# Two matmuls instead of three for the modulation of a gated recurrence: the high and low weight columns in one tile of 34, the pairs of rows added by ScalarE and VectorE

## The reference

```
x = x + L0(x)     # gated recurrence, the layer of the change
x = x + L1(x)     # one linear layer per sequence, weights chosen by index
x = x + L2(x)     # adapter with layernorm, weights chosen by index
x = x + L3(x)     # one linear layer per sequence, weights chosen by index

def L0(x):        # E = 512 channels, D = 2 traces
    ctx      = causal_ema(x, tau_ctx)
    wg       = sigmoid([x, ctx] @ Wg.T + bg)
    gated    = x * wg
    h1       = gelu(x @ Wn1.T + bn1)                 # 128 channels
    mod      = 0.5 + sigmoid(h1 @ Wn2.T + bn2)       # D = 2 values a token
    traces   = causal_ema(gated * mod[..., d], tau_d)   for d in 0, 1
    temporal = sum over d of traces[d] * softmax(blend)[d]
    gate     = sigmoid(temporal @ Wtemp.T + btemp)
    soma     = gelu(x @ Wsoma.T + bsoma)
    return layernorm((soma * gate) @ Wout.T)
```

## Time and profile before

| | |
|---|---|
| median of 3 runs | 731.97 us (731.63 to 732.11) |
| the profiled execution's own time | 731.42 us |
| its span, first to last instruction | 729.6 us |
| granted TensorE clock over the span | 1.000 of full speed (the 2.4 GHz level) |
| PE busy | 721.6 us, 99% |
| DVE busy | 539.2 us, 74% |
| ACT busy | 371.7 us, 51% |
| POOL busy | 121.6 us, 17% |
| DMA, mean over the span | 128 GB/s |

### The profile page before, as it was taken

How to read it: one execution, slowest core, us unless ns; L and a number is a source line. 1 busy time by engine, 2 the same in 40 slices (tenths; PEclk the granted TensorE clock), 3 DMA queues, 4 the chain that set the end, 5 groups by cost and what they waited for, 6 DMA issues and landing times. The chain is left out here.

```text
span 729.6 us, 10095 instructions
## 1 busy us (share of the span) xinstructions
PE 721.6 (99%) x3317; PEld 594.9 (82%) x3317; DVE 539.2 (74%) x808; ACT 371.7 (51%) x554; POOL 121.6 (17%) x220
## 2 busy tenths in 40 slices
PE   9999999999999999999999999999999999999998
PEld 8887888888888888888888888888887878888886
DVE  5799796695596597587578569875988687677583
ACT  4365446445535535545544543656566475374540
POOL 2000030031013004004004015205212012021110
PEclk9999999999999999999999999999999999999999
DMA  7959307935943962960980861724444636433312
GB/s 201 256 126 180 61 1 110 192 75 91 191 94 66 193 115 50 180 144 17 184 173 0 155 221 50 267 99 162 146 134 153 167 99 197 123 112 98 87 73 86
DMA packets 119310, 93.54 MB, mean 128 GB/s; under 512 B 75583, under 2 KB 103262, under 8 KB 117230
## 3 DMA queue, kind: packets, MB, share of 16 engines
q1 hardware_dynamic: 112718, 86.56, 49.7%
q10 hardware_dynamic: 6368, 6.59, 3.1%
q0 software_dynamic: 192, 0.00, 0.1%
HBM read 32.28 MB, written 25.20 MB: 79 GB/s over the span
## 5 line engine op out<-in xcount | busy, mean ns | idle before, releaser
L685 PE MATMUL pc<-x_h,wg_h 128*128 128x512 f32 x224 | 87.5, 391 | 1.2 <-DVE s_l L1766 1.1
L687 PE MATMUL pc<-x_h,wg_l 128*128 128x512 f32 x224 | 87.2, 389 | 0.0
L686 PE MATMUL pc<-x_l,wg_h 128*128 128x512 f32 x224 | 87.2, 389 | 0.0
L1565 DVE TENSOR_TENSOR_SCAN stage_b<-alpha,carry,stage_b 128x512 f32<-128x512 f32 x64 | 78.5, 1268 | 0.0
L685 PEld LDWEIGHTS pc<-x_h,wg_h 128*128 128x128 f32 x224 | 42.1, 188 | 11.6 <-issue 1.6
L1198 ACT ACTIVATE ctx_t<-ctx_t,col_all 128x512 f32<-128x512 f32 x32 | 23.2, 724 | 54.9 <-DVE ctx_t L1545 54.8
L803 PE MATMUL pm<-t_h,wt_h 128*128 128x512 f32 x128 | 50.2, 392 | 0.6 <-DVE t_l L1578 0.5
L685 PE MATMUL pm<-wo_h,s_h 128*128 128x512 f32 x128 | 50.0, 390 | 0.0
L805 PE MATMUL pm<-t_h,wt_l 128*128 128x512 f32 x128 | 49.9, 390 | 0.0
L804 PE MATMUL pm<-t_l,wt_h 128*128 128x512 f32 x128 | 49.8, 389 | 0.0
L687 PE MATMUL pm<-wo_h,s_l 128*128 128x512 f32 x128 | 49.8, 389 | 0.0
(11 more groups left out here) (280 smaller groups left out, 1880.1 us busy)
## 6 DMA issues: line engine op xcount, KB each, us to landing
x_planes<-x_pairs SPq DMA_DIRECT2D x56, 256.0 KB, 6.9
xt_scratch<-x_t SPq DMA_DIRECT2D x8, 1024.0 KB, 9.9
n_scratch<-stage_a SPq DMA_DIRECT2D x8, 1024.0 KB, 9.5
ctx_t<-xt_scratch SPq DMA_DIRECT2D x16, 512.0 KB, 7.1
x_pairs<-n_scratch SPq DMA_DIRECT2D x14, 512.0 KB, 6.0
out_dram<-x_tok SPq DMA_DIRECT2D x28, 256.0 KB, 2.4
mod<-mod_scratch ACTq DMA_DIRECT2D x8, 512.0 KB, 3.6
x_planes<-stage_b SPq DMA_DIRECT2D x60, 64.0 KB, 2.0
```

Of the source, the lines that this page charges most:

```text
L685: nc.tensor.matmul(acc, ah, bh, start=start and q == 0, stop=False)
L686: nc.tensor.matmul(acc, ah, bl, start=False, stop=False)
L687: last = nc.tensor.matmul(acc, al, bh, start=False, stop=stop and q == n - 1)
L1565: nc.vector.tensor_tensor_scan(tr[:, m % 2, :], alpha[:, 1 + d:2 + d].to_broadcast([P, BLK]), tr[:, m % 2, :], carry[:, D - d, m:m + 1], A ...
```

## The change

The weights of the modulation, two columns, are laid into one tile `wn2` of 34 columns: the high parts in columns 0 and 1, zeros in 2 to 31, the low parts in 32 and 33. One matmul with the high part of the hidden activation and one with its low part then give 34 rows of `pt[0]`: rows 0 and 1 hold what the high weights give, rows 32 and 33 what the low weights give (now also low by low, which was left out before). ScalarE copies rows 32 and 33 to `h1` (`mod_low`), VectorE adds rows 0 and 1 to them (`mod_add`), and `mod_tanh` works on the sum in `h1`. `h1_product` of the next block waits for that sum instead of the tanh. VectorE waits for `ident` near its start, since the zeros are made from it.

```
-        wn2_h, wn2_l = sb("wn2_h", [P, D], F32R), sb("wn2_l", [P, D], F32R)
+        wn2 = sb("wn2", [P, 32 + D], F32R)
...
+        mod_part, mod_sum = sem("mod_part"), sem("mod_sum")
...
             def h1_product(i):
...
-                after(pe, mod_raw, i)
+                after(pe, mod_sum, i)
...
             def mod_product(i):
                 pe.wait_ge(h1_hi, i + 1)
                 pe.wait_ge(h1_lo, i + 1)
-                product(pt[0][0:D, :], [(wn2_h[:, :], wn2_l[:, :], h_h[:, :], h_l[:, :])]).then_inc(mod_mm, 1)
+
+                rows = pt[0][0:32 + D, :]
+                nc.tensor.matmul(rows, wn2[:, :], h_h[:, :], start=True, stop=False)
+                nc.tensor.matmul(rows, wn2[:, :], h_l[:, :], start=False, stop=True).then_inc(mod_mm, 1)
...
+            def mod_low(i):
+
+                act.wait_ge(mod_mm, i + 1)
+                nc.scalar.activation(h1[0:D, :], pt[0][32:32 + D, :], ACT.Identity).then_inc(mod_part, 1)
+
             def mod_tanh(i):
 
-                act.wait_ge(mod_mm, i + 1)
-                nc.scalar.activation(h1[0:D, :], pt[0][0:D, :], ACT.Tanh, bias=col_bn2[0:D, 0:1],
+                act.wait_ge(mod_sum, i + 1)
+                nc.scalar.activation(h1[0:D, :], h1[0:D, :], ACT.Tanh, bias=col_bn2[0:D, 0:1],
                                      scale=0.5).then_inc(mod_raw, 1)
...
             def step(i, last=False):
                 gates(i - 1, lambda: hidden(i))
+                mod_low(i)
                 mod_tanh(i)
...
+            mod_low(0)
             mod_tanh(0)
...
-            gates(0, lambda: (mod_tanh(1), mod_to_dram(1)))
+            gates(0, lambda: (mod_low(1), mod_tanh(1), mod_to_dram(1)))
...
+            def mod_add(i):
+                dve.wait_ge(mod_part, i + 1)
+                nc.vector.tensor_tensor(h1[0:D, :], pt[0][0:D, :], h1[0:D, :], ALU.add).then_inc(mod_sum, 1)
+
...
             def step(i, last=False):
                 gates(i - 1, lambda: hidden_lo(i))
-                for c in range(NC):
-                    scan_context(i, c)
+                scan_context(i, 0)
+                scan_context(i, 1)
+                mod_add(i)
+                scan_context(i, 2)
+                scan_context(i, 3)
                 traces_part(i, last)
...
+            dve.wait_ge(setup_done, 1)
...
-            nc.vector.tensor_scalar(wn2_h[:, :], col_wn2[:, :], 1.0, None, ALU.mult).then_inc(setup_v, 1)
-            dve.wait_ge(setup_v, 9 + D)
-            nc.vector.tensor_tensor(wn2_l[:, :], col_wn2[:, :], f32(wn2_h[:, :]), ALU.subtract).then_inc(consts_v, 1)
+            nc.vector.tensor_scalar(wn2[:, 0:D], col_wn2[:, :], 1.0, None, ALU.mult).then_inc(setup_v, 1)
+            nc.vector.tensor_scalar(wn2[:, D:32], ident[:, D:32], 0.0, None, ALU.mult).then_inc(setup_v, 1)
+            dve.wait_ge(setup_v, 10 + D)
+            nc.vector.tensor_tensor(wn2[:, 32:32 + D], col_wn2[:, :], f32(wn2[:, 0:D]), ALU.subtract).then_inc(consts_v, 1)
             for c in range(NC):
                 scan_context(0, c)
+                if c == 1:
+                    mod_add(0)
                 prepare_behind(BEHIND_U, c)
...
-            gates(0)
+            gates(0, lambda: mod_add(1))
```

## The result

The changed kernel takes 734.07 us (median of 11 runs, 733.38 to 734.80), the kernel before 731.75 beside it (11 runs, 730.41 to 733.35). The ratio is 1.0033, with a 95% interval of 1.0024 to 1.0041: slower by 2.3 us. Forecast were 733.3 and a range of 731.5 to 734.9.

The account below looks back on a forecast made before the run. PE was taken to bound the kernel, with VectorE setting its pace in block 0 and level in block 1. 1.17 + 1.52 - 1.38 = +1.31 on 731.42, plus 0.55 to the median, gave 733.3; range 731.5 to 734.9.

Parts of the forecast that it names:

- Block 0, +1.17 forecast: Block 0: added steps and hand-overs, 1.41, less 0.23 for earlier matmuls, delay ScalarE's weight copies and PE: +1.17.
- block 1, +1.52: Block 1: the tanh starts 1.47 later and takes 0.05 more, so s_h, s_l and the VectorE chain come 1.52 later.
- Blocks 2 to 7: Blocks 2 to 7: mod_add costs nothing, the broadcast stays in place, PE gains 0.23 in six blocks: -1.38.
- the third rival: Blocks 2 to 6: the write lands later with its issue; 1.18 more once (734.5), 5.9 in all five (739.2); chance 0.12.
- the prediction's own signs of being wrong: No new wait in blocks 0 and 1, new PE waits for normalise1 in blocks 2 to 7, or granted clock under 1.00.
- The fourth rival: Block 7: the next layer's weights load and land later, delaying z_tanh, t_h and VectorE; 1.33 over forecast, 734.6; chance 0.09.
- the forecast's own range: Whole kernel: 732.8 to 734.0 around the forecast, from small errors in steps, hand-overs and matmul gains, without the rivals.
- The first rival: Blocks 0 and 1: neither chain binds, both delays are absorbed, all eight matmuls count: 1.84 gained, 730.13; chance 0.07.

Follow-up runs that it names:

- the run with the loads in the middle: Changed kernel with block 7's two x_pairs loads issued behind the n_scratch store, still ahead of the next layer's weights: 733.33 us, ratio 1.0019.
- the run over 2 columns: Changed kernel with two matmuls over only the 2 high columns, tanh straight from PSUM, no mod_low or mod_add: 729.25 us, beside 731.88 before.
- the pair over 34 columns: Changed kernel with its two matmuls over 34 columns, tanh straight from PSUM, mod_low and mod_add left out: 730.36 us, ratio 0.9991.
- three moves: Changed kernel, blocks 0 and 1 work moved ahead of the modulation path, block 7's x_pairs loads behind the weights: 728.91 us; kernel before, moved likewise: 731.29.

## Why the prediction came out as it did

**Block 0, +1.17 forecast (its terms give 1.18), +1.09 found; block 1, +1.52 and +1.51.** The terms were right one by one: mod_low 0.59 for 0.60, mod_add 0.68, tanh 0.72, hand-overs 0.03 to 0.04. That these steps are the cause is shown twice: the old path in these blocks takes both away, and the steps with three matmuls bring both back. Moving the queued work ahead of them removes them as well, which names the mechanism: what counted was the work queued behind the path on ACT, not the modulation itself.

**The step that failed is "Blocks 2 to 7", -1.38.** It was made of two claims.

The first, that in the loop the broadcast stays where it was because the write leaves behind the turned load anyway, held. The write of block 2 now takes 3.23 to the broadcast, 135.76 to 138.99, in place of 4.77. The turned load that the prediction meant is SP's DMA_TRANSPOSE; it is here first in the changed kernel, then in the kernel before:

```profile
132.24 4.80 SPq L339 DMA_TRANSPOSE x_pairs<-in_x_dram  x1
...
135.76 0.25 ACTq L1199 DMA_DIRECT2D mod_scratch<-h  x1
...
138.99 0.34 ACTq L1203 DMA_DIRECT2D mod<-mod_scratch  x1
```

```profile
130.09 4.85 SPq L338 DMA_TRANSPOSE x_pairs<-in_x_dram  x1
```

The broadcast goes out 1.95 and 2.01 behind the end of that issue (137.04 and 134.94), and 1.91 to 2.02 behind it in all five blocks of the loop, in both kernels, whenever the write was issued. No run moved this load, so that it holds the write back is read from the order in time. ACT's waits for these landings have shrunk from 9.6:

```profile
ACT stage_a L1118 <- DMA mod_scratch<-h: 4.1, 5, 1.5
```

So the later issue was absorbed by a wait that had been there, and the third rival is out. The Trainium skill, page "DMA: Bandwidth & Descriptors", section "Queues, rings and completion order", has each DMA engine take packets from its queues in turn. The prediction had concluded from it that the write would move with its issue. That conclusion did not hold here: the broadcast kept its 1.91 to 2.02 behind SP's load. Only the size was off: 0.19 a block where the price of one matmul, 0.23, was put, 0.87 in the five blocks of this execution instead of 1.15. In the seven intervals behind the pair the matmuls lie 0.228 to 0.236 apart instead of 0.227, which takes back 0.03.

The second claim carried this over to block 7, and that failed: +1.20 in place of -0.23. In block 7 the queues carry other transfers. The broadcast was 1.45 ahead of the x_pairs loads; the later write, and 0.44 more from write to broadcast, took it 1.67 later against the modulation matmul, and the loads came 0.76 earlier against it, so the order turned by 2.43. The later modulation is enough for that: in the run with the path of before in blocks 0 and 1 the loads leave 5.01 behind the matmul, as in the kernel before (5.05), and the broadcast, 5.62 behind it, still stands behind them and takes 7.2 to land. PE's wait of 1.41 for normalise1 in block 7 is one of the prediction's own signs of being wrong. The fourth rival had the place and nearly the size (1.33 more than forecast, 1.43 found), but not the mechanism: in the changed kernel the weights' loads are issued 1.23 later against the matmul, yet the weights reach wg_h no later than before (17.91 behind the matmul, before 18.13, 418.88 to 437.01 in the earlier trace rows). The run with the loads in the middle shows that they are nearly as tight: 0.7 later, and DVE waits 0.82.

**The sum.** +1.17 + 1.52 - 1.38 = +1.31 was forecast, +1.09 + 1.51 - 0.87 + 1.20 = +2.93 found in the blocks. The time, 734.07, lies just above the forecast's own range of 732.8 to 734.0. It fell into the stated range all the same, by luck: in the part that the third and fourth rivals had opened, through a loss that neither of them described.

**Gain and loss add up.** With neither edit the blocks take 448.20, with the matmul out alone 446.53 (the run over 2 columns), with the steps alone 452.72, with both 451.13. So the matmul brings 1.67 or 1.59, and the steps cost 4.52 (1.30, 1.45 and 1.77 in blocks 0, 1 and 7) or 4.60. The 1.67 rests on one execution; the pair over 34 columns has 448.26, with its 1.19 of waiting for Wtemp and 0.28 more in block 1. The first rival's 1.84 is nearly reached, but only without the steps.

**Open.** Why the matmuls behind a pair are spaced wider than behind three; why the loads of block 7 came 0.76 earlier against the matmul (two issues of SP ahead of them, seq_gamma and seq_beta, took 2.25 and 0.60 instead of 2.99 and 1.04); the 1.19 of waiting for Wtemp in one execution; why POOL's step takes 1.51 in some kernels and 2.11 in others.

## What to carry to other kernels

A step added to a short path costs what is queued behind it on the engines that run in order: in two of eight blocks that was work which PE needed, in five it was a wait that was there anyway. A block with a different program, here the last with its transfers for the next layer, needs a budget of its own, since a transfer that leaves 1.7 later may find another one ahead of it and land 3.6 later still. If a step must be added, move what stands behind it ahead of it: the same change was slower by 2.3 us in its place and faster by 2.2 with three moves, of which, in the traces, 0.8 belong to the moves alone and 1.5 to the matmul.

## What was not expected of the hardware

Behind two matmuls over 2 or 34 columns the next came 0.228 to 0.236 apart for seven intervals, behind three 0.227, with or without readers of the bank. In block 7 a 512 KB broadcast issued 0.61 to 1.21 behind two loads of 512 KB on another queue took 7.2 to 7.4 to land (three kernels), ahead of them 3.8 to 4.1, without them 3.5 to 4.1. And the first product began 8.84 to 9.63 into the span in the kernels profiled here, so a single span does not tell differences under 1 us; lengths of blocks with the same program and no wait of their own repeat to 0.1.
